# Keeping the last sums of four head pairs in SBUF until they are rotated, in place of their PSUM banks

## The chip, the cores and the metric

The kernel runs on one core of a Trainium2 chip. The metric is the time of one execution on the device, in microseconds (us). Engines are named as the profile names them: PE (TensorE matmul), DVE (VectorE), ACT (ScalarE), POOL (GpSimd) and SP (SyncE, which here only issues DMAs). SBUF is the on-chip memory that all of them read; PSUM has eight banks of 128 x 512 fp32, which PE writes and from which DVE and ACT read.

## What is computed

The reference is two gated blocks, each a cross attention and a feed-forward, on x of 8 x 256 tokens by 1024. The change touches one stage of the second attention, the queries:

```python
q = (query @ wq).reshape(bs, s, N_Q_HEADS, D_K).transpose(0, 2, 1, 3)   # 32 heads of 128
q = _rope(q)                                                           # x*cos + rot(x)*sin
```

`query` is the layer-normalised x (2048 x 1024), `wq` is 1024 x 4096. Everything is fp32 in and out; each fp32 product is made of three matmuls on split high and low parts.

## The kernel before, in words

Each engine has its own program, and the programs meet only in semaphores. `weave` interleaves the stages; the query stage, written once as `qp_schedule` and played by one class per engine, runs from 1021 to 1657 us of the profile. Before it comes the first feed-forward (names f0), after it the attention proper (names at).

The 32 heads are taken two at a time (a pair, 16 of them), once for each half of the tokens: pairs 0 to 15 for the first half, 16 to 31 for the second. A pair's query projection is one step of a Strassen-Winograd scheme, so seven products i = 0 to 6, of 12 matmuls each (`product`, the matmuls are lines 150 to 152 in the helper `three`), each into one PSUM bank. The banks are used in a ring of eight (`qp_bank`), so a product waits until the bank of the product eight places before it is read for the last time (`qp_emptied`).

`sum` adds the products up. ACT copies product 0 into c11 (line 2140). DVE adds product 1 into c12 (2163), 2 into c21 (2166), 3 into c12 (2169), and at line 2174 products 3, 4, 5, 6 give the four result quarters. c11, c12, c21 and c22 are SBUF tiles, two of each, pair modulo 2. Where line 2174 writes is told by `qp_sum`: for the last two pairs an SBUF tile of the pair, for product 3 of a coupled pair c22, otherwise back into the product's own bank.

`turn(pair, tn, part)` is the rotary embedding of one token half-block (tn 0: the quarters 4 and 5; tn 1: 6 and 3). It is six DVE instructions of 128 x 512: two products of the upper quarter with cosine and sine (2188, 2189), two of the lower one (2192, 2194, which write back over the quarters), a difference (2196) and a sum (2198) into qp_r. SP then stores qp_r. The tables qp_rope and the result qp_r lie in SBUF. So a turn reads, beside SBUF, whatever place `qp_sum` gave.

Most pairs are worked through one by one. Pairs (0, 1), (14, 15), (16, 17) and (30, 31) are coupled: their products alternate, pair by pair, because the x operands arrive then (at the begin) or are exchanged for the other token half (14 to 17). In the same stretches DVE splits the x operands (`expand`, line 2150, 128 x 1024, both inputs in SBUF). A block's turns with tn 0 are queued on DVE behind product 5's sums, those with tn 1 behind product 6's; DVE takes them in this order:

```python
if i > 4 and block[-1] < LASTP:
    for pair in block:
        for part in range(3):
            do.turn(pair, i - 5, part)
```

POOL prepares the weights of the products to come, six ahead (`prepare`): it forms the sums and differences of the weight blocks (2214, 2216, 2224, 2228) and the low parts (2220), all from SBUF to SBUF.

Of the kernel before, what the change touches and what calls it, by code (L numbers as in the profile page):

```python
# [92 lines left out]
class Signals:  # L93
# [14 lines left out]
    def inc(self, name, key, step=1):  # L108
        if self.counting:
            assert (name, key) not in self.value, (name, key)  # L110
            self.total[name] = self.total.get(name, 0) + step
            self.value[name, key] = self.total[name]
        return self.sem(name), step
# [4 lines left out]
    def at(self, name, key):  # L118
        if self.counting:
            return self.sem(name), 1  # L120
        return self.sem(name), self.value[name, key]
# [41 lines left out]
def flamingo(nc, x, ctx, ctxT, mask, gates, w0T, b0, agT, bT, gb, wq, wk, wv, wo,  # L163
             w1T, b1, enc, coef, cmask, tab, four, rope, ident, out):
    es = ExitStack()
    with es:
        sig = Signals(nc, es)
        at, inc, landed = sig.at, sig.inc, sig.landed
# [16 lines left out]
        def place(name, kb, shape, dt=F):  # L185
            return nc.alloc_sbuf_tensor_at(name, shape, dt, offset=BASE + int(1024 * kb))
# [1757 lines left out]
        NP = H // 2  # L1944
        LASTP = 2 * NP - 1
# [4 lines left out]
        Q_ORDER = [(pair, i) for block in Q_BLOCKS for i in range(7) for pair in block]  # L1950
        Q_TURNS = [(pair, tn) for block in Q_BLOCKS for tn in range(2) for pair in block]
        Q_COUPLED = [pair for block in Q_BLOCKS for pair in block if len(block) > 1]
        qp_ring = [place(f"qp_a{i}", kb, [P, 2, 4, P], R) for i, kb in enumerate((48, 52, 60, 64, 68, 72, 201.25))]
        qp_x = [[place(f"qp_b{i}_{k}", kb, [P, 2, 2, 512], R) for k, kb in enumerate(kbs)] for i, kbs in enumerate((
            (187, 0), (155, 171), (163, 179), (8, 84), (112, 120), (128, 136), (144, 104)))]
# [11 lines left out]
        def qp_bank(pair, i):  # L1967
            j = qp_at(pair, i)
            return 5 + j % 3 if pair >= LASTP - 1 else (0, 1, 4, 5, 6, 7, 2, 3)[j % 8]

        def qp_sum(pair, i):

            if pair >= LASTP - 1 or (i == 3 and pair in Q_COUPLED):
                return {3: qp_c22, 4: qp_c11, 5: qp_c21, 6: qp_c12}[i][pair % 2][:, :]
            return BK[qp_bank(pair, i)]

        def qp_emptied(pair, i):
            if i == 0:
                return ("qp_act", ("sum", pair, 0))
            if i < 3 or pair >= LASTP - 1 or (i == 3 and pair in Q_COUPLED):  # L1980
                return ("qp_dve", ("sum", pair, i))
            return ("qp_dve", {3: ("q1", pair, 1), 4: ("q0", pair, 0), 5: ("q1", pair, 0), 6: ("q0", pair, 1)}[i])

# [89 lines left out]
        class QpTensor(Queries):  # L2073
# [3 lines left out]
            def product(self, pair, i):  # L2077
                on, b, sb = self.on, qp_bank(pair, i), pair // NP
                for e in self.spare[b]:
                    on.wait_ge(*at(*e))  # L2080
                self.spare[b] = [qp_emptied(pair, i)]
                on.wait_ge(*at("qp_act", ("w", pair, i)))
                on.wait_ge(*at("qp_pool", ("w", pair, i)))
                w = qp_ring[qp_at(pair, i) % NR]
                for k in range(2):
                    x = qp_x[i][k]
                    on.wait_ge(*at("qp_act", ("x", sb, i, k)))
                    on.wait_ge(*at("qp_dve", ("x", sb, i, k)))
                    for c in range(2):
                        m = three(self.pe, BK[b], (w[:, 0, 2 * k + c, :], w[:, 1, 2 * k + c, :]), (x[:, 0, c, :], x[:, 1, c, :]),  # L2090
                                  k + c == 0, k + c == 2)
                m.then_inc(*inc("qp_pe", ("M", pair, i)))

        class QpScalar(Queries):
# [40 lines left out]
            def sum(self, pair, i):  # L2135
                if i == 0:
                    self.on.wait_ge(*at("qp_pe", ("M", pair, 0)))
                    if pair > 1:
                        self.on.wait_ge(*at("qp_dve", ("sum", pair - 2, 6)))
                    self.act.activation(qp_c11[pair % 2][:, :], BK[qp_bank(pair, 0)], ACT.Copy).then_inc(*inc("qp_act", ("sum", pair, 0)))  # L2140

        class QpVector(Queries):
# [10 lines left out]
            def sum(self, pair, i):  # L2153

                dve, on = self.dve, self.on
                c11, c12, c21 = (a[pair % 2][:, :] for a in (qp_c11, qp_c12, qp_c21))
                if i == 0:
                    return
                m = BK[qp_bank(pair, i)]
                on.wait_ge(*at("qp_pe", ("M", pair, i)))  # L2160
                if i == 1:
                    on.wait_ge(*at("qp_act", ("sum", pair, 0)))
                    dve.tensor_tensor(c12, c11, m, ALU.add).then_inc(*inc("qp_dve", ("sum", pair, 1)))
                if i == 2:
                    on.wait_ge(*at("qp_dve", ("sum", pair, 1)))
                    dve.tensor_tensor(c21, c12, m, ALU.add).then_inc(*inc("qp_dve", ("sum", pair, 2)))
                if i == 3:
                    on.wait_ge(*at("qp_dve", ("sum", pair, 2)))
                    dve.tensor_tensor(c12, c12, m, ALU.add).then_inc(*inc("qp_dve", ("fourth", pair)))
                    on.wait_ge(*at("qp_dve", ("fourth", pair)))  # L2170
                if i == 6:
                    on.wait_ge(*at("qp_dve", ("fourth", pair)))
                if i > 2:
                    dve.tensor_tensor(qp_sum(pair, i), {3: c21, 4: c11, 5: c21, 6: c12}[i], m, ALU.add).then_inc(*inc("qp_dve", ("sum", pair, i)))  # L2174

            def turn(self, pair, tn, part):

                dve, on, n = self.dve, self.on, Q_TURNS.index((pair, tn))
                top, low, q0, q1 = (a.rearrange("p (s n) -> p s n", s=4) for a in (
                    qp_sum(pair, (4, 6)[tn]), qp_sum(pair, (5, 3)[tn]), qp_r[n % 2][0][:, :], qp_r[n % 2][1][:, :]))  # L2180
                if part == 0:
                    on.wait_ge(*at("qp_rope", 1))
                    on.wait_ge(*at("qp_dve", ("sum", pair, (5, 6)[tn])))
                    if n > 1:
                        on.wait_ge(*at(f"qp_s{n % 2}", Q_TURNS[n - 2] + (1, 1)))
                    else:
                        on.wait_ge(*at("f0_xos", (NT // 2 - 1, 5)))
                    dve.tensor_tensor(q0, top, qp_angle(0, tn), ALU.mult)  # L2188
                    dve.tensor_tensor(q1, top, qp_angle(1, tn), ALU.mult).then_inc(*inc("qp_dve", ("top", pair, tn)))  # L2189
                if part == 1:  # L2190
                    on.wait_ge(*at("qp_dve", ("top", pair, tn)))
                    dve.tensor_tensor(top, low, qp_angle(1, tn), ALU.mult).then_inc(*inc("qp_dve", ("sine", pair, tn)))  # L2192
                    on.wait_ge(*at("qp_dve", ("sine", pair, tn)))
                    dve.tensor_tensor(low, low, qp_angle(0, tn), ALU.mult).then_inc(*inc("qp_dve", ("low", pair, tn)))  # L2194
                if part == 2:
                    dve.tensor_tensor(q0, q0, top, ALU.subtract).then_inc(*inc("qp_dve", ("q0", pair, tn)))  # L2196
                    on.wait_ge(*at("qp_dve", ("low", pair, tn)))
                    dve.tensor_tensor(q1, q1, low, ALU.add).then_inc(*inc("qp_dve", ("q1", pair, tn)))  # L2198
# [1042 lines left out]
```

## Time and profile before

| | |
|---|---|
| three timed runs | 3001.97 us median (2999.51 to 3003.76) |
| the profiled execution | 3001.45 us |
| its span on the core | 2999.7 us |
| PE busy | 2963.3 us, 99% |
| DVE busy | 2013.1 us, 67% |
| ACT busy | 1282.9 us, 43% |
| POOL busy | 1368.7 us, 46% |
| granted PE clock | 1.00 in the query stage (2.4 GHz) |

Busy is the time in which an engine ran an instruction; PE with 99% has about 36 us without one, in the whole kernel. A row of a timeline has start, duration, engine, line and tiles, and in brackets how long the engine stood idle before it and for whom. Durations of neighbouring DVE rows overlap by about 0.08 us, so the step from start to start is what an instruction costs in a queue.

### The profile page before, as it was taken

Reading aid. Unit: us, or ns where it says so; the run is one execution under the profiler, and the core shown is the slowest. Engines: PE = TensorE matmul, PEld = TensorE weight load, DVE = VectorE, ACT = ScalarE, POOL = GpSimd, SP = SyncE. Lnnn points to the kernel's source line nnn. Section 1 sums busy time; section 2 is a strip of 40 time slices with the busy share of each in tenths; the row PEclk is TensorE's granted clock in tenths of the full one; section 3 lists DMA queues with packets and bytes.
Section 4 is the critical chain, followed back from the end, with each engine's and each line's share of the span. In section 5 each row is a group of like instructions: output and inputs, shape, how many; then the busy total and the mean of one; then the engine's idle time right before and its main releaser. Section 6 shows DMA issues by size and latency. Waiting matters only on the chain.

```text
span 2999.7 us, 41114 instructions
## 1 busy us (share of the span) xinstructions
PE 2963.3 (99%) x14701; PEld 2484.3 (83%) x14701; DVE 2013.1 (67%) x4714; ACT 1282.9 (43%) x2686; POOL 1368.7 (46%) x1105
## 2 busy tenths in 40 slices
PE   9999999999999999999999999999999999999999
PEld 7888878887788878887888888888888888888887
DVE  4432478888655686679666777666766676666566
ACT  4111366665322422232224565555555545544332
POOL 2422388896422577778776433322222211111254
PEclk9999999999999999999999999999999999999999
DMA  7332421212655654455444776766677666665531
GB/s 253 127 120 98 172 64 50 78 64 74 201 172 176 194 164 113 113 155 158 110 110 136 243 256 227 243 218 211 190 224 241 191 193 202 209 191 165 225 112 71
DMA packets 320661, 488.29 MB, mean 163 GB/s; under 512 B 26236, under 2 KB 155644, under 8 KB 317644
## 3 DMA queue, kind: packets, MB, share of 16 engines
q1 hardware_dynamic: 319740, 484.23, 50.8%
q8 instruction: 118, 1.93, 0.3%
q10 hardware_dynamic: 720, 1.44, 0.1%
q14 instruction: 83, 0.68, 0.1%
HBM read 324.12 MB, written 161.48 MB: 162 GB/s over the span
## 4 chain that ended last, share of the span: by engine, by line
PE 59%; DVE 4%; DMA 0%; POOL 0%; ACT 0%; issue 0%; SPq 0%; DVEq 0%; ACTq 0%
PE PB L150 18%; PE PB L151 18%; PE PB L152 18%; PE PB L2400 4%; DVE qp_b L2150 1%; PE PB L2825 0%; DVE PB L2192 0%; DMA qp_raw<-in_wq 0%; DVE qp_r L2198 0%; DVE PB L2174 0%; DVE qp_c L2194 0%; DVE at_bi L2506 0%; DVE qp_r L2188 0%; DVE qp_r L2189 0%; DVE at_ptl L2539 0%
## 5 line engine op out<-in xcount | busy, mean ns | idle before, releaser
L2562 POOL TENSOR_TENSOR at_ql<-at_qf,at_qh 128x512 fp32r<-128x512 f32 x128 | 166.2, 1299 | 843.9 <-ACT at_qh L2440 843.9
L2447 ACT ACTIVATE at_ss<-at_ss,at_sm,at_bs 128x256 f32<-128x256 f32 x512 | 301.9, 591 | 318.1 <-DVE at_sm L2523 318.1
L150 PE MATMUL PB<-at_woh,at_ah 128*128 128x512 f32 x1024 | 400.8, 391 | 0.6 <-DVE at_al L2545 0.6
L151 PE MATMUL PB<-at_wol,at_ah 128*128 128x512 f32 x1024 | 400.2, 391 | 0.0
L152 PE MATMUL PB<-at_woh,at_al 128*128 128x512 f32 x1024 | 399.4, 390 | 0.0
L2553 DVE SCALAR_TENSOR_TENSOR at_xt<-PB,gt,at_xt 128x512 f32<-128x512 f32 x256 | 192.1, 751 | 255.7 <-PE PB L152 255.7
L150 PE MATMUL PB<-qp_b,qp_a 128*128 128x512 f32 x896 | 349.4, 390 | 7.2 <-DVE qp_r L2196 2.7
L152 PE MATMUL PB<-qp_b,qp_a 128*128 128x512 f32 x896 | 348.7, 389 | 0.0
L151 PE MATMUL PB<-qp_b,qp_a 128*128 128x512 f32 x896 | 348.7, 389 | 0.0
L2220 POOL TENSOR_TENSOR qp_a<-qp_raw,qp_a 128x512 fp32r<-128x512 f32 x192 | 259.2, 1361 | 100.6 <-ACT qp_a L2112 97.9
L2112 ACT ACTIVATE qp_a<-qp_raw 128x512 fp32r<-128x512 f32 x192 | 113.4, 626 | 295.3 <-POOL qp_raw L2224 162.6
L2459 ACT ACTIVATE at_pth<-PB 128x512 fp32r<-128x512 f32 x256 | 139.3, 596 | 231.8 <-PE PB L2400 231.8
L152 PEld LDWEIGHTS PB<-at_woh,at_al 128*128 128x128 f32 x1024 | 192.5, 188 | 41.1
L150 PEld LDWEIGHTS PB<-at_woh,at_ah 128*128 128x128 f32 x1024 | 193.1, 189 | 37.6 <-ACT at_ah L2470 0.8
L151 PEld LDWEIGHTS PB<-at_wol,at_ah 128*128 128x128 f32 x1024 | 193.0, 188 | 35.2
L150 PEld LDWEIGHTS PB<-qp_b,qp_a 128*128 128x128 f32 x896 | 168.2, 188 | 44.7 <-DVE qp_r L2196 3.5
L152 PEld LDWEIGHTS PB<-qp_b,qp_a 128*128 128x128 f32 x896 | 168.2, 188 | 35.1
L151 PEld LDWEIGHTS PB<-qp_b,qp_a 128*128 128x128 f32 x896 | 168.2, 188 | 34.7
L2539 DVE TENSOR_TENSOR at_ptl<-PB,at_pth 128x512 fp32r<-128x512 f32 x256 | 164.8, 685 | 39.5 <-ACT at_pth L2459 39.5
L2519 DVE CUSTOM_DVE_ANT_0 at_ss<-PB,at_bi 128x256 f32<-128x256 f32 x512 | 185.6, 419 | 0.8 <-PE PB L152 0.6
L150 PE MATMUL PB<-at_kh,at_qh 128*128 128x256 f32 x512 | 155.9, 305 | 0.0
L2533 DVE TENSOR_SCALAR at_ss<-at_ss,at_sm 128x256 f32<-128x256 f32 x512 | 150.7, 358 | 4.5
(314 smaller groups left out, 7579.3 us busy)
## 6 DMA issues: line engine op xcount, KB each, us to landing
at_woh<-wod SPq DMA_DIRECT2D x48, 1024.0 KB, 6.9
at_wol<-wod SPq DMA_DIRECT2D x48, 1024.0 KB, 9.5
qp_raw<-in_wq SPq DMA_DIRECT2D x32, 1024.0 KB, 5.4
qd<-qp_r SPq DMA_DIRECT2D x256, 128.0 KB, 2.5
at_qf<-qd SPq DMA_DIRECT2D x128, 256.0 KB, 3.4
at_rawo<-in_wo SPq DMA_DIRECT2D x32, 512.0 KB, 5.0
wod<-at_woh SPq DMA_DIRECT2D x16, 1024.0 KB, 5.5
wod<-at_wol SPq DMA_DIRECT2D x16, 1024.0 KB, 6.3
```

The lines of the kernel that those rows point to most:

```text
L150: pe.matmul(o, ah, bh, start=start, stop=False)
L151: pe.matmul(o, ah, bl, start=False, stop=False)
L152: return pe.matmul(o, al, bh, start=False, stop=stop)
L2220: pool.tensor_tensor(qp_part(pair, i, 1), qp_weight(pair, i), asf(qp_part(pair, i, 0)), ALU.subtract).then_inc(*inc("qp_pool", ("w", pair, ...
L2400: m = pe.transpose(PB[1][:, 512 * k + P * c:512 * k + P * c + P], at_ss[s][:, c, P * k:P * k + P], idt[:, :])
L2447: m = act.activation(at_ss[s][:, c, :], at_ss[s][:, c, :], ACT.Exp, bias=z[:, 4 + c:5 + c], scale=at_bs[:, qn % 2, 8 + 2 * b + c % 2:9 + 2 ...
L2459: self.act.activation(at_pth[:, k, :], BK[2 + k], ACT.Copy).then_inc(*inc("at_act", ("pt", u, k)))
L2519: dve.tensor_tensor_reduce(out=at_ss[s][:, c, :], in0=PB[0][:, L * c:L * c + L], in1=at_bi[qn % 2][:, 2 * b + c % 2, :], scale=1.0, scalar ...
L2533: dve.tensor_scalar(at_ss[s][:, c, :], at_ss[s][:, c, :], z[:, 12 + c:13 + c], None, ALU.mult).then_inc(*inc("at_dve", ("weight", u, c)))
L2539: self.dve.tensor_tensor(at_ptl[:, k, :], BK[2 + k], asf(at_pth[:, k, :]), ALU.subtract).then_inc(*inc("at_dve", ("pt", u, k)))
L2553: self.dve.scalar_tensor_tensor(out=xt, in0=BK[6 + p % 2], scalar=gt[:, 2:3], in1=xt, op0=ALU.mult, op1=ALU.add).then_inc(*inc("at_dve", ( ...
L2562: self.pool.tensor_tensor(at_ql[n % 3][:, :], at_qf[n % 2][:, :], asf(at_qh[n % 3][:, :]), ALU.subtract).then_inc(*inc("at_pool", ("q", n)))
```

## The change

A tuple `Q_KEPT` names the pairs 0, 1, 14, 15 and the last two, 30 and 31. For those, `qp_sum` now gives the SBUF tiles c22, c11, c21 and c12, where it did so before for 30 and 31 (and, of the coupled pairs, for product 3). A bank of such a pair is then free with the sum that reads it, and not with the turn's last reading. Since c11, c12 and c21 hold results until the turn is over, the pair two further on (which has the same tiles) waits for it: ACT's copy for q0 of tn 0, DVE's sums 1 and 3 for q0 and q1 of tn 1. No instruction is added, removed or moved.

```diff
+        Q_KEPT = (0, 1, NP - 2, NP - 1, LASTP - 1, LASTP)
...
         def qp_sum(pair, i):
 
-            if pair >= LASTP - 1 or (i == 3 and pair in Q_COUPLED):
+            if pair in Q_KEPT or (i == 3 and pair in Q_COUPLED):
                 return {3: qp_c22, 4: qp_c11, 5: qp_c21, 6: qp_c12}[i][pair % 2][:, :]
             return BK[qp_bank(pair, i)]
 
         def qp_emptied(pair, i):
             if i == 0:
                 return ("qp_act", ("sum", pair, 0))
-            if i < 3 or pair >= LASTP - 1 or (i == 3 and pair in Q_COUPLED):
+            if i < 3 or pair in Q_KEPT or (i == 3 and pair in Q_COUPLED):
                 return ("qp_dve", ("sum", pair, i))
...
                     if pair > 1:
-                        self.on.wait_ge(*at("qp_dve", ("sum", pair - 2, 6)))
+                        self.on.wait_ge(*at("qp_dve", ("q0", pair - 2, 0) if pair - 2 in Q_KEPT else ("sum", pair - 2, 6)))
...
                 on.wait_ge(*at("qp_pe", ("M", pair, i)))
+                if i in (1, 3) and pair - 2 in Q_KEPT:
+                    on.wait_ge(*at("qp_dve", (("q0", "q1")[i // 2], pair - 2, 1)))
```

On DVE, the last sums of the couple (0, 1) and the first turn of pair 0. Before (c110 and c210 are c11 and c21 of the even pair, c111 and c211 of the odd one, PB0 and PB2 hold banks):

```order
950 L2174 TENSOR_TENSOR PB0<-qp_c110_187,PB0 128x512 [waits qp_pe]
951 L2174 TENSOR_TENSOR PB0<-qp_c111_188,PB0 128x512 [waits qp_pe]
952 L2174 TENSOR_TENSOR PB2<-qp_c210_191,PB2 128x512 [waits qp_pe]
953 L2174 TENSOR_TENSOR PB2<-qp_c211_192,PB2 128x512 [waits qp_pe]
954 L2188 TENSOR_TENSOR qp_r00_195<-PB0,qp_rope_186 128x512 [waits f0_xos,qp_dve,qp_rope]
955 L2189 TENSOR_TENSOR qp_r01_196<-PB0,qp_rope_186 128x512
956 L2192 TENSOR_TENSOR PB0<-PB2,qp_rope_186 128x512 [waits qp_dve]
957 L2194 TENSOR_TENSOR PB2<-PB2,qp_rope_186 128x512 [waits qp_dve]
958 L2196 TENSOR_TENSOR qp_r00_195<-qp_r00_195,PB0 128x512
```

The same place of DVE in the changed kernel (its line numbers are 4 higher here):

```order
950 L2178 TENSOR_TENSOR qp_c110_187<-qp_c110_187,PB0 128x512 [waits qp_pe]
951 L2178 TENSOR_TENSOR qp_c111_188<-qp_c111_188,PB0 128x512 [waits qp_pe]
952 L2178 TENSOR_TENSOR qp_c210_191<-qp_c210_191,PB2 128x512 [waits qp_pe]
953 L2178 TENSOR_TENSOR qp_c211_192<-qp_c211_192,PB2 128x512 [waits qp_pe]
954 L2192 TENSOR_TENSOR qp_r00_195<-qp_c110_187,qp_rope_186 128x512 [waits f0_xos,qp_dve,qp_rope]
955 L2193 TENSOR_TENSOR qp_r01_196<-qp_c110_187,qp_rope_186 128x512
956 L2196 TENSOR_TENSOR qp_c110_187<-qp_c210_191,qp_rope_186 128x512 [waits qp_dve]
957 L2198 TENSOR_TENSOR qp_c210_191<-qp_c210_191,qp_rope_186 128x512 [waits qp_dve]
958 L2200 TENSOR_TENSOR qp_r00_195<-qp_r00_195,qp_c110_187 128x512
```

The order and the count are the same; the places have changed. A sum reads one SBUF tile and one bank as before and writes SBUF; the turn's instructions had a bank among their inputs and now have two inputs in SBUF.

## Rows read from the trace of the kernel before

**Rows 1.** The page: the span, and PE's busy time, share and instructions.

```profile
span 2999.7 us, 41114 instructions
...
PE 2963.3 (99%) x14701; PEld 2484.3 (83%) x14701; DVE 2013.1 (67%) x4714; ACT 1282.9 (43%) x2686; POOL 1368.7 (46%) x1105
```

**Rows 2.** Timeline of PE, the query stage's waits: start, us, instruction, idle before.

```profile
1094.73 0.50 PE L150 MATMUL PB<-qp_b,qp_a 128*128 128x512 f32 x1 [2.30 <-DVE qp_r L2198]
...
1348.81 0.50 PE L150 MATMUL PB<-qp_b,qp_a 128*128 128x512 f32 x1 [0.82 <-DVE qp_r L2196]
1353.68 0.50 PE L150 MATMUL PB<-qp_b,qp_a 128*128 128x512 f32 x1 [1.85 <-DVE qp_r L2196]
...
1364.28 0.50 PE L150 MATMUL PB<-qp_b,qp_a 128*128 128x512 f32 x1 [2.14 <-DVE qp_c L2163]
```

**Rows 3.** Timeline of DVE, from the first turn of pair 0 on.

```profile
1059.87 0.68 DVE L2188 TENSOR_TENSOR qp_r<-PB,qp_rope 128x512 f32<-128x512 f32 x1
...
1063.71 0.68 DVE L2188 TENSOR_TENSOR qp_r<-PB,qp_rope 128x512 f32<-128x512 f32 x1
...
1068.76 0.68 DVE L2188 TENSOR_TENSOR qp_r<-PB,qp_rope 128x512 f32<-128x512 f32 x1
...
1070.08 1.79 DVE L2192 TENSOR_TENSOR PB<-qp_c,qp_rope 128x512 f32<-128x512 f32 x1
1071.90 1.66 DVE L2194 TENSOR_TENSOR qp_c<-qp_c,qp_rope 128x512 f32<-128x512 f32 x1
1073.48 0.68 DVE L2196 TENSOR_TENSOR qp_r<-qp_r,PB 128x512 f32<-128x512 f32 x1
...
1075.18 0.68 DVE L2188 TENSOR_TENSOR qp_r<-PB,qp_rope 128x512 f32<-128x512 f32 x1
...
1081.94 0.68 DVE L2163 TENSOR_TENSOR qp_c<-qp_c,PB 128x512 f32<-128x512 f32 x1
...
1094.00 0.68 DVE L2198 TENSOR_TENSOR qp_r<-qp_r,PB 128x512 f32<-128x512 f32 x1
```

**Rows 4.** Timeline of POOL beside the turns with tn 1 of pair 0.

```profile
1070.01 3.00 POOL L2220 TENSOR_TENSOR qp_a<-qp_raw,qp_a 128x512 fp32r<-128x512 f32 x2
1072.97 1.74 POOL L2214 TENSOR_TENSOR qp_s<-qp_raw 128x512 f32<-128x512 f32 x1
```

**Rows 5.** All instructions on qp_c, by form: ns min/median/max, first and last start.

```profile
L2194 DVE TENSOR_TENSOR qp_c<-qp_c,qp_rope x10: 691/1654/1702, 1071.9 to 1752.7; 128x512 f32<-128x512 f32 x10
...
L2192 DVE TENSOR_TENSOR PB<-qp_c,qp_rope x6: 699/1522/1787, 1070.1 to 1386.5; 128x512 f32<-128x512 f32 x6
L2188 DVE TENSOR_TENSOR qp_r<-qp_c,qp_rope x4: 684/684/693, 1660.6 to 1742.9; 128x512 f32<-128x512 f32 x4
```

**Rows 6.** Timeline of DVE, from the first turn of pair 14 on.

```profile
1332.12 0.68 DVE L2188 TENSOR_TENSOR qp_r<-PB,qp_rope 128x512 f32<-128x512 f32 x1
...
1339.81 2.91 DVE L2150 TENSOR_TENSOR qp_b<-qp_in,qp_b 128x1024 fp32r<-128x1024 f32 x2
...
1343.84 0.68 DVE L2188 TENSOR_TENSOR qp_r<-PB,qp_rope 128x512 f32<-128x512 f32 x1
...
1350.59 0.70 DVE L2192 TENSOR_TENSOR PB<-qp_c,qp_rope 128x512 f32<-128x512 f32 x1
...
1354.63 9.00 DVE L2150 TENSOR_TENSOR qp_b<-qp_in,qp_b 128x1024 fp32r<-128x1024 f32 x4
1363.55 1.27 DVE L2163 TENSOR_TENSOR qp_c<-qp_c,PB 128x512 f32<-128x512 f32 x2
```

**Rows 7.** Timeline of POOL beside it.

```profile
1351.20 1.27 POOL L2220 TENSOR_TENSOR qp_a<-qp_raw,qp_a 128x512 fp32r<-128x512 f32 x1 [3.59 <-ACT qp_a L2112]
...
1358.17 7.84 POOL L2220 TENSOR_TENSOR qp_a<-qp_raw,qp_a 128x512 fp32r<-128x512 f32 x4
```

**Rows 8.** Busy us (x instructions) of PE, PEld, DVE, ACT, POOL in the turns' two stretches.

```profile
1059.80:1081.95 22.15, 22.15 (x98) 18.04 (x98) 21.87 (x28) 7.02 (x13) 20.14 (x16) 1.00 0.36 73
1332.10:1354.70 22.60, 19.93 (x87) 15.86 (x86) 22.32 (x30) 12.20 (x18) 14.06 (x12) 1.00 0.62 162
```

## The prediction, made before the changed kernel ran

> **What bounds the kernel now.** I read the page first: PE is busy 99% of the span [rows 1]. A change off PE can give back only PE's idle time, but whatever makes PE wait longer is paid in full. So the second view was PE's timeline in the query stage, looking for brackets with idle time. There are four of weight [rows 2]: 2.30 us at 1094.73, then 0.82, 1.85 and 2.14 us between 1348 and 1365, together 7.1 us. All four wait for DVE. This is the most that the change can gain.
>
> Third, DVE's timeline before each wait, to see what it was late with. At the first place DVE runs without a pause from the first turn of pair 0 at 1059.87 to 1094.00 [rows 3], where L2198 is q1 of pair 2's turn tn 1, and PE starts 0.05 us after that instruction's end. This product, (3, 4), wants the bank of (2, 3). Pair 2 is not kept, so this wait is not removed; everything that DVE does between 1059.87 and 1094.68 stands in front of it. At the second place the waits at 1348.81 and 1353.68 are for q0 of the turns of pairs 14 and 15, whose banks the change frees. The last, at 1364.28, is for the sum 1 of pair 16 (L2163, first of two from 1363.55 [rows 6]), which is queued behind all turns of 14 and 15 and four L2150. It stays too.
>
> Fourth, how long one DVE instruction takes by where its inputs lie. A turn with bank inputs steps evenly: six instructions from 1059.87 to 1063.71, 3.84 us or 0.64 each [rows 3]. With two inputs in SBUF there are two prices. The four L2188 at the kernel's tail take 0.684 us, so two SBUF inputs are not dear in themselves. L2194 on c22 has a median of 1.654 and a maximum of 1.702, L2192 from c22 goes from 0.699 to 1.787 [rows 5]. The cheap case of L2192 is that at 1350.59 [rows 6], in a gap in which POOL had been idle for 3.59 us until 1351.20 [rows 7]. The dear ones, 1.79 and 1.66 us at 1070.08 and 1071.90 [rows 3], lie beside a POOL that works without a gap; POOL's two instructions take 3.00 us there and the next 1.74 [rows 4]. In between, at 1073.48, an instruction with a bank input takes 0.68 again, with POOL still running. So an instruction of DVE with both inputs in SBUF and one of POOL take turns, and an instruction with one input in a bank goes past.
>
> **The change part by part.** No instruction is added. The sums (L2174) read one bank as before; only their target moves, and L2163, which reads a bank and writes an SBUF tile, takes 0.68 us [rows 3], as the turns on banks do. I put them at 0, with a bound of some hundredths of a us each way.
>
> The turns of pairs 0, 1, 14 and 15 are eight, 48 instructions. Now 12 of them read two SBUF inputs (L2192, L2194 and L2198 of tn 1, four turns); after the change all 48 do. Beside a working POOL I price one at 1.66 us, the row at 1071.90, so a turn at 6 x 1.66 = 9.96 us.
>
> First place. The turns with tn 0 take 3.84 us each now, so 2 x (9.96 - 3.84) = 12.2 more. Those with tn 1 take 6.42 (1068.76 to 1075.18) and 6.76 (1075.18 to 1081.94) [rows 3], so 19.92 - 13.18 = 6.7 more. Sum 18.9 if each one meets POOL. POOL is busy 20.14 of 22.15 us there [rows 8], 91%; its gaps and the moment when its ring of seven weight buffers is full, while PE stands, lower this. I take 85%: 16 us. Bounds: 0 (no meeting) and 18.9. PE now has no slack at 1094.73, it waits already, so the 16 us pass to it whole. PE will stand earlier as well: product (3, 2) wants the bank of (2, 1), freed by the sum that now starts at 1081.94 and would start at 1098.
>
> Second place. Turns with tn 0 now take 1332.12 to 1339.81, 7.69 us for two, so 19.92 - 7.69 = 12.2 more; those with tn 1 take 10.79 us for two (1343.84 to 1354.63 [rows 6]), so 9.1 more, 21.4 in all if each meets POOL. But POOL is busy only 14.06 of 22.60 us, 62%, with 12 instructions [rows 8]. By the share it would be 13.3 us. By the count: each POOL instruction can be met once, some 5 of the 12 are met now (the slow ones of tn 1 and one L2150), 7 are left, 7 x 1.06 = 7.4 (1.06 is from 1.70, the row's upper value, less 0.64). I take 9 us, nearer to the count, because a DVE that takes longer finds no more POOL work than there is until PE goes on. Bounds: 0 and 21.4. The wait at 1364.28 is for DVE, so this too passes whole. The two bank waits that go, 0.82 and 1.85 us, give nothing, since PE then stands at the later one, for a DVE that is later still.
>
> The new waits: ACT's copy of (2, 0) into c11 waits for q0 of pair 0's turn tn 0. Queued behind it on ACT are the weight copies of products to come; DVE reaches q0, its fifth instruction, about 5 x 1.02 = 5 us later than now, which costs at most a us or two of the lead of six products. The waits before DVE's sums 1 and 3 are for DVE's own earlier instructions, in queue order already: 0. SP's stores of qp_r come later with the turns, and the weight load behind them with them; a load is asked for seven products before its use, so I put this at 0, with up to some us if that cover is gone.
>
> Sum: 16 + 9 = 25 us on the profiled execution's 3001.45 us (span 2999.7), so 3026.5. The median of the runs, 3001.97, lies 0.5 above the profiled one. I predict 3026 us. Bounds of all: 7.1 us faster if nothing is dearer and every wait goes, 40 us slower if every instruction meets POOL.
>
> The row at 1071.90 shows DVE and POOL alternating with 1.66 us for a pair. The Trainium skill, "SBUF — State Buffer", section "Who interferes with whom", says that a DVE instruction with two SBUF inputs contends with a GpSimd instruction that reads SBUF, for the whole of the instruction, and that one with a single SBUF input does not contend. It speaks against this change, and the trace agrees on both kinds. By its "whole instruction" a meeting would cost the full length of a POOL instruction, 1.27 us [rows 7] beside 0.64, so 1.91 for a DVE instruction, and the sum would be about 30 us; the rows say 1.66, and I go by them.
>
> **The rivals.**
> A, the forecast: 18 to 34 us slower, 3019 to 3035.
> B, the meetings starve themselves. PE stands, so POOL's ring stays full and POOL is idle for half of the turns. Half of the first place (9) and a third of the second (3) give 12 us, 3013; it covers 3008 to 3019. For it: at 1351.20 POOL was idle 3.59 us in just this way. Against it: in the first place POOL is the busier side.
> C, POOL falls behind as well. Each meeting lengthens its instruction, by 1.74 - 1.27 = 0.47 or less [rows 4, 7]; 40 of them cost it up to 19 us, and PE waits for weights on top of DVE. 25 + 15 gives 3042, from 3035 on. Against it: PE waits for no weights now.
> D, the change does what it says and DVE is not slowed: the banks are free with the sums, 0.82 + 1.85 go and with luck all 7.1 us; 2994 to 2999. It would need SBUF inputs at 0.68 us beside a busy POOL. The tail's rows speak for it, those at 1070 against it.
> E, DVE is slowed but the wait at 1094.73 is not behind it, and time stays within 6 us. Against it is the unbroken row of DVE work up to 1094.
>
> **How the numbers follow.** A 0.65, B 0.16, C 0.08, D 0.06, E 0.05. A measurement of this kernel can tell about 0.2%, 6 us, from no change. Faster by more than that needs D at its best, 0.03; within it are the rest of D and E, 0.08; slower 0.89. The range 3009 to 3037 takes in A, most of B and the near end of C, and leaves out D, E and the far end of C, under 0.2.
>
> **What would show it.** In the profile after: the turns of pairs 0, 1, 14, 15 (L2192 to L2202 there) with inputs from qp_c at a median near 1.65 us between 1060 and 1100 and mixed between 1335 and 1380; the sum 1 of pair 2 (L2167) starting near 1098 in place of 1081.94; PE idle of about 18 us before (3, 4), in two or three waits for qp_c and qp_r, and about 14 us at the second place; POOL's instructions beside the turns at 1.6 to 1.75 us. Nothing after 1400 us should be changed but shifted. I am wrong if the turns stay near 0.68 us beside a working POOL (then D), if PE waits for POOL or ACT at these places (C), or if the turns are dear but PE's total wait in the stage stays under some 15 us (B).

## The result, and the profile after

| | before | after |
|---|---|---|
| timed runs, median | 3001.40 us (2999.51 to 3003.76, 5 runs) | 3027.42 us (3027.07 to 3029.36, 5 runs) |
| profiled execution, its span | 3001.45, 2999.7 us | 3027.07, 3025.3 us |

The ratio after to before is 1.0088, with a 95% interval of 1.0077 to 1.0099: the change makes the kernel 26 us slower. Predicted were 3026 us and a range of 3009 to 3037. Line numbers of the changed kernel are as before up to 1952; ACT's lines and `expand` (2152) are 2 higher; DVE's sum (2167 to 2178 in place of 2163 to 2174), its turn (2192 to 2202 in place of 2188 to 2198) and POOL's lines are 4 higher.

The page of the changed kernel: same counts, 24 us more of DVE, 7 of POOL, 8 of PE.

```profile
span 3025.3 us, 41115 instructions
...
PE 2971.2 (98%) x14701; PEld 2489.1 (82%) x14701; DVE 2036.8 (67%) x4714; ACT 1282.9 (42%) x2686; POOL 1375.5 (45%) x1105
```

PE's timeline in the query stage, all stops of weight, beside those of [rows 2]:

```profile
1066.38 0.47 PE L150 MATMUL PB<-qp_b,qp_a 128*128 128x512 f32 x1 [1.03 <-POOL qp_a L2224]
...
1097.68 0.79 PE L150 MATMUL PB<-qp_b,qp_a 128*128 128x512 f32 x1 [9.23 <-DVE qp_c L2167]
1109.75 0.79 PE L150 MATMUL PB<-qp_b,qp_a 128*128 128x512 f32 x1 [4.68 <-DVE qp_r L2202]
1110.34 0.63 PE L151 MATMUL PB<-qp_b,qp_a 128*128 128x512 f32 x1
1110.77 0.63 PE L152 MATMUL PB<-qp_b,qp_a 128*128 128x512 f32 x1
...
1368.69 0.50 PE L150 MATMUL PB<-qp_b,qp_a 128*128 128x512 f32 x1 [2.71 <-DVE qp_c L2178]
...
1377.02 0.47 PE L150 MATMUL PB<-qp_b,qp_a 128*128 128x512 f32 x1 [2.59 <-ACT qp_a L2114]
1388.64 0.80 PE L150 MATMUL PB<-qp_b,qp_a 128*128 128x512 f32 x1 [4.29 <-DVE qp_c L2167]
```

7.1 us of waits have become some 25 (the first row's 1.03 us for POOL included). The stop at 1094.73 now ends at 1109.75, 15.0 us later, with one more before it; that at 1364.28 ends at 1388.64, 24.4 later. And a matmul takes 0.63 us behind the long stops, with 0.43 from start to start.

DVE's timeline at the first place, against [rows 3], the first turn of pair 0 and the start of pair 1's, the start of the turns with tn 1, and the end of the stretch:

```profile
1060.20 0.77 DVE L2192 TENSOR_TENSOR qp_r<-qp_c,qp_rope 128x512 f32<-128x512 f32 x1
1060.89 1.77 DVE L2193 TENSOR_TENSOR qp_r<-qp_c,qp_rope 128x512 f32<-128x512 f32 x1
1062.70 1.67 DVE L2196 TENSOR_TENSOR qp_c<-qp_c,qp_rope 128x512 f32<-128x512 f32 x1
1064.40 0.69 DVE L2198 TENSOR_TENSOR qp_c<-qp_c,qp_rope 128x512 f32<-128x512 f32 x1
1065.01 1.77 DVE L2200 TENSOR_TENSOR qp_r<-qp_r,qp_c 128x512 f32<-128x512 f32 x1
1066.70 1.78 DVE L2202 TENSOR_TENSOR qp_r<-qp_r,qp_c 128x512 f32<-128x512 f32 x1
1068.41 1.78 DVE L2192 TENSOR_TENSOR qp_r<-qp_c,qp_rope 128x512 f32<-128x512 f32 x1
...
1079.80 1.83 DVE L2192 TENSOR_TENSOR qp_r<-qp_c,qp_rope 128x512 f32<-128x512 f32 x1
...
1095.75 0.68 DVE L2200 TENSOR_TENSOR qp_r<-qp_r,qp_c 128x512 f32<-128x512 f32 x1
1096.35 0.68 DVE L2202 TENSOR_TENSOR qp_r<-qp_r,qp_c 128x512 f32<-128x512 f32 x1
1096.96 0.67 DVE L2167 TENSOR_TENSOR qp_c<-qp_c,PB 128x512 f32<-128x512 f32 x1
```

POOL beside it:

```profile
1060.39 1.74 POOL L2224 TENSOR_TENSOR qp_a<-qp_raw,qp_a 128x512 fp32r<-128x512 f32 x1
1062.20 1.62 POOL L2228 TENSOR_TENSOR qp_raw<-qp_s,qp_raw 128x512 f32<-128x512 f32 x1
1064.63 3.31 POOL L2224 TENSOR_TENSOR qp_a<-qp_raw,qp_a 128x512 fp32r<-128x512 f32 x2 [0.81 <-ACT qp_a L2114]
...
1092.02 3.26 POOL L2224 TENSOR_TENSOR qp_a<-qp_raw,qp_a 128x512 fp32r<-128x512 f32 x2
1104.45 1.28 POOL L2218 TENSOR_TENSOR qp_s<-qp_raw 128x512 f32<-128x512 f32 x1 [9.16 <-DMA qp_raw<-in_wq]
```

The pattern is the one of [rows 3] and [rows 4], now on 19 of the 24 instructions of the four turns: about 1.7 us from start to start beside a working POOL, both engines lengthened. The row at 1064.40 is one of the exceptions and fits the pattern: POOL's instruction of 1062.20 has ended at 1063.82 and its next starts at 1064.63, and DVE takes 0.69. The same at 1095.75, after POOL's last instruction at 1095.28. The sum 1 of pair 2 starts at 1096.96 in place of 1081.94.

### The profile page after: what moved, and what is told of

Read it like the earlier page. It is cut to its first block, busy times and chain, and to the rows that moved or that the text cites. A ratio compares the mean times of both kernels' runs of the same rounds, so it can differ in the third digit from the quotient of the medians.

```text
span 3025.3 us, 41115 instructions
## 1 busy us (share of the span) xinstructions
PE 2971.2 (98%) x14701; PEld 2489.1 (82%) x14701; DVE 2036.8 (67%) x4714; ACT 1282.9 (42%) x2686; POOL 1375.5 (45%) x1105
## 4 chain that ended last, share of the span: by engine, by line
PE 59%; DVE 5%; DMA 1%; issue 0%; ACT 0%; POOL 0%; SPq 0%; DVEq 0%; ACTq 0%
PE PB L150 18%; PE PB L151 18%; PE PB L152 18%; PE PB L2404 4%; DVE qp_b L2152 1%; DVE qp_r L2193 0%; PE PB L2829 0%; DVE qp_r L2192 0%; DVE qp_r L2202 0%; DVE qp_c L2196 0%; DVE qp_c L2198 0%; DMA qp_raw<-in_wq 0%; DVE qp_r L2200 0%; DVE at_bi L2510 0%; DVE f1st L2942 0%
## 5 line engine op out<-in xcount | busy, mean ns | idle before, releaser
L150 PEld LDWEIGHTS PB<-qp_b,qp_a 128*128 128x128 f32 x896 | 170.2, 190 | 64.3 <-DVE qp_c L2167 14.4
L152 PEld LDWEIGHTS PB<-qp_b,qp_a 128*128 128x128 f32 x896 | 170.3, 190 | 35.9
L151 PEld LDWEIGHTS PB<-qp_b,qp_a 128*128 128x128 f32 x896 | 170.4, 190 | 35.3
```

The lines of the kernel that those rows point to most:

```text
L150: pe.matmul(o, ah, bh, start=start, stop=False)
L151: pe.matmul(o, ah, bl, start=False, stop=False)
L152: return pe.matmul(o, al, bh, start=False, stop=stop)
```

## The experiments

The theory: a DVE instruction with two SBUF inputs waits for a POOL instruction that reads SBUF, and the reverse; the change turns 36 more instructions into that kind at two places where DVE is what PE waits for. Rivals: two SBUF inputs are dear in themselves; the new waits hold an engine up; the early free banks change PE's order of work for the worse. A second theory came from the profile after: PE's clock is lower for some us behind the long stops, and that is a cost of its own. The kernel before was timed anew beside each group of experiments, so its median is 3001.98, 3001.16 or 3002.91 us below.

**Each place alone.**

```diff
-        Q_KEPT = (0, 1, NP - 2, NP - 1, LASTP - 1, LASTP)
+        Q_KEPT = (0, 1, LASTP - 1, LASTP)                    # e1_first
+        Q_KEPT = (NP - 2, NP - 1, LASTP - 1, LASTP)          # e2_second
```

> Only pairs 0 and 1 (beside 30 and 31) are kept in SBUF; pairs 14 and 15 as before. Theory (dearer turns, then a slow PE clock behind the stall): 15.0 us of later DVE plus 2.3 us of slow matmuls, so 17 us slower than before, near 3018.5, and nothing at 1330 to 1400 us. Rival (the first place is off the bound): under 6 us. Rival (one common cause such as the longer program or the memory layout): all 26 us here too.

Measured: 3018.13 us against 3001.98, ratio 1.0053 (1.0041 to 1.0066), 16.2 us slower, as the theory said.

> Only pairs 14 and 15 (beside 30 and 31) are kept. Theory: the rest of the change's cost, 7.0 us of later DVE plus 2.8 us of slow matmuls behind the stall, so 8 to 10 us slower than before, near 3011; the two together give the whole change. If the places interact (the first shifting what meets what at the second), the two differences do not add up to 26.

Measured: 3009.91 against 3001.98, ratio 1.0028 (1.0018 to 1.0038), 7.9 us slower. 16.2 + 7.9 = 24.1, within the intervals the 26.0 of both. The two places stand for the whole, the first with two thirds.

**The free bank taken back.** The sums stay in SBUF, but PE waits for the banks until the turns are over.

```diff
-            if i < 3 or pair in Q_KEPT or (i == 3 and pair in Q_COUPLED):
+            if i < 3 or pair >= LASTP - 1 or (i == 3 and pair in Q_COUPLED):      # in qp_emptied
```

> The changed kernel, but PE waits for a kept pair's banks until its turns are over, as before the change. The SBUF inputs of the turns stay. Theory (the inputs are the cost, the early free bank gives nothing because PE stands for DVE in any case): within 3 us of the changed kernel, 3025 to 3030. Rival (the early bank gives back a part, the inputs cost more than was seen): 3033 or more. Rival (the early start of PE is what collides): near 3001.

Measured: 3021.52 against 3001.98, ratio 1.0067 (1.0052 to 1.0082). None of the three: it is 19.5 us slower than before, where the changed kernel is 26.0 slower. So three quarters of the loss come with the inputs alone, and the early bank makes it worse by some 6 us, not better. The size is rough: the two kernels were not timed side by side, and the intervals of their ratios overlap. PE's timeline of this kernel, its two long stops at the first place and its last one at the second:

```profile
1076.21 0.52 PE L150 MATMUL PB<-qp_b,qp_a 128*128 128x512 f32 x1 [4.86 <-DVE qp_r L2200]
...
1094.72 0.79 PE L150 MATMUL PB<-qp_b,qp_a 128*128 128x512 f32 x1 [5.05 <-DVE qp_r L2200]
...
1384.96 0.50 PE L150 MATMUL PB<-qp_b,qp_a 128*128 128x512 f32 x1 [2.73 <-DVE qp_c L2167]
```

PE stands earlier (at the bank of pair 0's quarter) and its last stop at the first place ends at 1094.72, not at 1109.75. The slow matmuls behind that stop run while DVE is still catching up, and PE reaches the critical product (3, 4) when its bank is just free. In the changed kernel PE runs ahead through the freed banks, then stands for DVE twice, the second time at (3, 4) itself, and the slow matmuls behind that stop are on the path. DVE's stretch is also 1 us shorter here (1059.46 to 1107.94 against 1060.20 to 1109.70) and begins 0.7 us earlier. At the second place DVE's part is the same in both (7.1 and 7.0 us), but here the last stop is 2.73 us long and the clock stays at 1.00 behind it, where the changed kernel has a stop of 4.29 us and a fall of the clock. Behind the second place this kernel is 20.7 us later than the one before and the changed one 27.2, so 6.5 us apart. Of its 27.2 us the changed kernel lost 5.2 behind its two last stops, at the lower clock (2.4 and 2.8, worked out below); this one lost 0.3 there. That the early bank costs mainly by way of the clock is read from one execution of each and was not tried by itself.

**The changed waits alone**, on the kernel before:

```diff
-                        self.on.wait_ge(*at("qp_dve", ("sum", pair - 2, 6)))
+                        self.on.wait_ge(*at("qp_dve", ("q0", pair - 2, 0) if pair - 2 in (0, 1, NP - 2, NP - 1) else ("sum", pair - 2, 6)))
...
+                if i in (1, 3) and pair - 2 in (0, 1, NP - 2, NP - 1):
+                    on.wait_ge(*at("qp_dve", (("q0", "q1")[i // 2], pair - 2, 1)))
```

> The kernel before with the change's two new waits alone (ACT's copy for q0 of tn 0, DVE's sums 1 and 3 for q0 and q1 of tn 1, of the pair two before, for pairs 0, 1, 14, 15). Sums stay in their banks. Theory: the waits cost nothing, within 2 us of before. Rival (ACT held by the wait delays the weight copies queued behind it, and PE waits for weights): 3 to 10 us slower.

Measured: 3002.71 against 3001.98, ratio 1.000 (0.9991 to 1.0009). The waits cost nothing that shows: by the interval, under 3 us. ACT's is not even a further wait. The kernel before waits at the same place for sum 6 of the pair two before, and DVE takes that sum behind q0 of tn 0, so the edit lets ACT's copy go earlier. For pair 16, first before, then with the edit:

```profile
1343.42 0.60 ACT L2140 ACTIVATE qp_c<-PB 128x512 f32<-128x512 f32 x1 [3.13 <-DVE PB L2174]
...
1341.99 0.58 ACT L2140 ACTIVATE qp_c<-PB 128x512 f32<-128x512 f32 x1
```

The profiled execution with the edit has two short waits of PE that the one of before lacks, 0.98 us for POOL at 1376.76 and 0.50 us for ACT at 1380.23. No run shows where they come from.

**POOL without its reads.** For the weights of pairs 0 to 5 and 13 to 19 POOL writes zeros in place of the low parts, sums and differences, in the kernel before (e5) and in the changed one (e6).

```diff
+                op = (lambda o, a, b, f: pool.memset(asf(o), 0.0)) if pair <= 5 or NP - 3 <= pair <= NP + 3 else pool.tensor_tensor
...
-                pool.tensor_tensor(qp_part(pair, i, 1), qp_weight(pair, i), asf(qp_part(pair, i, 0)), ALU.subtract).then_inc(
+                op(qp_part(pair, i, 1), qp_weight(pair, i), asf(qp_part(pair, i, 0)), ALU.subtract).then_inc(
```

> The kernel before, with POOL's work on the weights of pairs 0 to 5 and 13 to 19 (low parts, sums and differences) left out: POOL writes zeros to the same tiles and reads nothing from SBUF. Theory (a DVE instruction with two SBUF inputs waits for a POOL instruction that reads SBUF): the slow L2192, L2194, L2198 and L2150 become fast, 0.69 and 1.2 us, DVE's backlog shrinks and PE's 7 us of waits in the stage go, so 5 to 8 us faster than before, 2994 to 2997. Rival (POOL's writes collide too): as before, 3001.

Measured: 2991.28 against 3001.16, ratio 0.9966 (0.9952 to 0.9979).

> The changed kernel with the same work of POOL left out (zeros written, nothing read, for the weights of pairs 0 to 5 and 13 to 19). Theory: the change's whole cost is the meeting with POOL's reads, so this is within 2 us of the same edit on the kernel before, 2994 to 2998, and all turns take 0.69 us an instruction. Rival (two SBUF inputs are dear in themselves, or the later write to c11, c12 and c21 holds someone): 20 to 26 us slower than the same edit on the kernel before.

Measured: 2991.40 against 3001.16, ratio 0.9965 (0.9951 to 0.9979). This is the deciding pair. With POOL's reads the change costs 26 us, without them 0.1. Both are faster than the kernel before by 10 us, and PE has no stop for DVE over 0.2 us left in the stage: the kernel before had been paying for such meetings too. The forms of the turns in the changed kernel with the zeros (min, median and max ns), against [rows 5]:

```profile
L2198 DVE TENSOR_TENSOR qp_c<-qp_c,qp_rope x14: 691/691/694, 1058.7 to 1743.3; 128x512 f32<-128x512 f32 x14
L2202 DVE TENSOR_TENSOR qp_r<-qp_r,qp_c x14: 681/684/687, 1059.9 to 1752.3; 128x512 f32<-128x512 f32 x14
L2192 DVE TENSOR_TENSOR qp_r<-qp_c,qp_rope x12: 680/684/692, 1056.7 to 1733.4; 128x512 f32<-128x512 f32 x12
```

and two neighbours in its timelines of DVE and of POOL, where POOL writes zeros while DVE reads two SBUF tiles:

```profile
1065.59 0.68 DVE L2192 TENSOR_TENSOR qp_r<-qp_c,qp_rope 128x512 f32<-128x512 f32 x1
...
1065.87 0.53 POOL L2212 MEMSET qp_s<- 128x512 f32 x1
```

The largest of these DVE durations is 0.694 us, and some of the instructions lie beside a memset, so a POOL instruction that only writes does not hold them. A limit of this test: a memset takes 0.53 us and not 1.29, so POOL is also idle for most of the time, and the times alone can't tell reads from mere work of POOL; the rows beside a memset can. The same rows show that two inputs in SBUF and a result in c11, c12 or c21 are not dear in themselves.

**DVE late without any meeting.** The kernel before, with the first instruction of pair 0's turn, on a bank, done 20 times more (e7) or 5 times more (e9).

```diff
+                    for k in range(20 if (pair, tn) == (0, 0) else 0):     # 5 in e9_delay_small
+                        dve.tensor_tensor(q0, top, qp_angle(0, tn), ALU.mult).then_inc(*inc("qp_more", k))
+                        on.wait_ge(*at("qp_more", k))
```

> The kernel before with DVE delayed at the first place and nothing else: the first instruction of pair 0's turn (one bank and one SBUF input, 0.6 to 0.75 us a step) is done 20 times more. Theory (DVE's backlog passes one to one to PE, and the stop adds some 2 us of slow PE clock): the added 12 to 15 us and 2 us, 14 to 17 us slower than before, with POOL's instructions near 1.29 us. Rival (DVE has slack and the change cost by POOL's lengthening): under 6 us slower.

Measured: 3016.94 against 3001.16, ratio 1.0051 (1.0036 to 1.0067), 15.8 us slower (by the interval, 11 to 20). In its trace:

```profile
1061.12 14.46 DVE L2189 TENSOR_TENSOR qp_r<-PB,qp_rope 128x512 f32<-128x512 f32 x20
...
1078.27 0.68 DVE L2199 TENSOR_TENSOR qp_r<-qp_r,PB 128x512 f32<-128x512 f32 x1
...
1096.19 0.68 DVE L2163 TENSOR_TENSOR qp_c<-qp_c,PB 128x512 f32<-128x512 f32 x1
```

```profile
1062.74 1.29 POOL L2227 TENSOR_TENSOR qp_raw<-qp_s,qp_raw 128x512 f32<-128x512 f32 x1
1064.84 2.55 POOL L2223 TENSOR_TENSOR qp_a<-qp_raw,qp_a 128x512 fp32r<-128x512 f32 x2 [0.81 <-ACT qp_a L2112]
```

POOL runs at 1.29 us beside DVE's bank instructions, and 14.5 us of DVE make the sum 1 of pair 2 14.25 us late and the span 13.4 us longer (3013.1 against 2999.7); this execution was the fastest of the four. So DVE's lateness at this place does pass to the end nearly in full, by itself, whatever made it. The 2 us for the clock are not in this trace: the clock fell behind a stop of 9.72 us at 1079.00, but PE stands for DVE once more behind it, 3.00 us until 1108.99, and after that stop the clock stayed up.

> The kernel before, with DVE delayed by 5 steps of 0.72 us (3.6 us) at the first turn of pair 0, on a bank and an SBUF input. Theory: PE waits 3.6 us more, in one stop of near 6 us, behind which its clock falls for some 2 us: 4 to 6 us slower than before, 3005 to 3007. Rival (PE had slack for small delays): no change.

Measured: 3004.70 against 3002.91, ratio 1.0009 (1.0000 to 1.0019), 1.8 us slower: less than expected. In the profiled execution the wait before 1095.55 grew by only 0.7 us, from 2.30 to 2.98. DVE's stretch began 1.3 us earlier there (an operand had come sooner), and the turns with tn 1, shifted against POOL, took 11.7 us in place of 13.2. In this execution a part of the delay was swallowed by meeting less, and the clock did not fall behind these stops.

**Looking for something better than before.** e8 keeps one more sum, product 3 of pair 2, in c22, so that the product which stood at 1094.73 has its bank.

```diff
-            if pair >= LASTP - 1 or (i == 3 and pair in Q_COUPLED):
+            if pair >= LASTP - 1 or (i == 3 and pair in Q_COUPLED + [2]):          # in qp_sum, and alike in qp_emptied
```

> The kernel before, with product 3 of pair 2 alone put into c22 as well (so that the bank of (2, 3) is free with its sum and not with q1 of the turn tn 1). Theory: the wait of 2.30 us at 1094.73 goes, for 1 to 3 us more of DVE time in the turn (three instructions with two SBUF inputs) which nobody waits for; 1 to 2.5 us faster than before, 2999 to 3001. Rival (the added meetings bring back a wait of the same length): no change, or 1 us slower.

Measured: 2998.76 against 3001.16, ratio 0.9990 (0.9982 to 0.9999): 2.4 us faster, just clear of 1, and as the theory said. In its trace the wait at 1094.73 is gone. The later ones are 0.92, 2.63 and 2.14 us, 0.9 us more than before. The profiled execution, 3002.65 us, is the slowest of its eleven, so it can't show where the 2.4 us were gained.

e10 goes the other way about and lets the turn read a bank where it had read c22: ACT copies it there.

```diff
+            def turn(self, pair, tn, part):                                        # QpScalar
+                if part == 0 and qp_swap(pair, tn):                                # tn 1 of 0, 1, 14 to 17
+                    self.on.wait_ge(*at("qp_dve", ("top", pair, tn)))
+                    self.act.activation(qp_sum(pair, 6), qp_sum(pair, 3), ACT.Copy).then_inc(*inc("qp_act", ("moved", pair)))
...
+                if part and qp_swap(pair, tn):                                     # QpVector.turn
+                    top, low = low, top
```

> The kernel before, with the meetings it had already made fewer: in the coupled blocks (0, 1), (14, 15) and (16, 17), ACT copies quarter 3 from c22 into the bank of quarter 6 once the turn has read that bank, DVE reads the copy, and the two pairs' turns with tn 1 take their parts alternately so that the copy is hidden. Of the three instructions of such a turn with two SBUF inputs one is left. Theory: about 3.5 us less of DVE time at the first place and 1 to 2 at the second, the wait of 2.30 us at 1094.73 goes and the later ones shrink: 2 to 5 us faster than before, 2996 to 2999. Rival (DVE waits for the copy as long as it saves): no change.

Measured: 3000.22 against 3002.91, ratio 0.9993 (0.9984 to 1.0002): 2.7 us faster, but unclear. The step worked where it was aimed: PE's waits for DVE are gone at both places, and the sum 1 of pair 2 starts at 1078.29. In their place stands one for POOL:

```profile
1348.67 0.76 PE L150 MATMUL PB<-qp_b,qp_a 128*128 128x512 f32 x1 [3.47 <-POOL qp_a L2236]
```

## Why the prediction was right

The time, the places and the mechanism came as written; the parts of the sum did not all have their size, and one was missing.

**First place, 16 us predicted.** DVE was 15.0 late at (3, 4), 109.70 - 94.68 in the trace's last digits. The turns with tn 0 took 18.4 us (1060.20 to 1078.60) in place of 7.7, so 10.7 more, of the 12.2 possible; those with tn 1 17.2 (1079.80 to 1096.96) in place of 13.2, so 4.0 of 6.7. The stretch also began 0.3 later. POOL's gaps were where I put them; a step was 1.70 us, a little over my 1.66. The share of 85% was 78%. PE stood 14.9 us there (1.03, 9.23 and 4.68), where I had named about 18.

**Second place, 9 us predicted.** Measured 7.0: the shift of PE grows from 17.4 (L2167 at 1321.88 against L2163 at 1304.51) to 24.4 at the stop of 1388.64. The turns with tn 0 took 7.5 us more. Those with tn 1 took 0.9 us less than before, not more, since POOL stood idle for 8.44 us until 1375.40. It waited for ACT's copies of weights, and these were queued behind ACT's copy of an x operand, for which ACT stood 7.49 us until its DMA had landed at 1372.80. By the program that DMA waits for a split of DVE's, which here ended at 1368.04. DVE itself, being late, had kept POOL idle:

```profile
1369.16 0.68 DVE L2192 TENSOR_TENSOR qp_r<-qp_c,qp_rope 128x512 f32<-128x512 f32 x1
...
1374.33 0.69 DVE L2196 TENSOR_TENSOR qp_c<-qp_c,qp_rope 128x512 f32<-128x512 f32 x1
...
1375.67 1.76 DVE L2200 TENSOR_TENSOR qp_r<-qp_r,qp_c 128x512 f32<-128x512 f32 x1
```

This is what the rival B forecast, POOL idle during the turns, at half of one place, though it came by a DMA and not by a full ring of weight buffers. The count of POOL's instructions (7.4) came nearer than its busy share (13.3), at this one place. PE stood 9.6 us here (2.71, 2.59 and 4.29), where I had named about 14.

**The term that was missing: PE's clock.** Behind a long stop the matmuls start 0.43 us apart in place of 0.23, for about a dozen of them. Busy times and, third from the end, the granted clock, of the changed kernel:

```profile
1110.00:1115.00 5.00, 5.00 (x13) 3.90 (x14) 2.37 (x4) 1.35 (x3) 3.76 (x3) 0.52 0.91 204
1115.00:1120.00 5.00, 5.00 (x24) 4.12 (x23) 2.75 (x5) 1.27 (x2) 3.87 (x3) 1.00 1.03 432
...
1389.00:1394.00 5.00, 5.00 (x13) 3.84 (x13) 4.93 (x9) 0.00 (x0) 1.36 (x2) 0.50 0.76 240
```

0.50 is the lower level, 1.2 GHz. At the first place this is 17.4 - 15.0 = 2.4 us, at the second 27.2 - 24.4 = 2.8 us (27.2 is the shift of the same sums at 1572.36 before and 1599.55 after). The prediction has no term for the clock and says that the stops pass whole; they pass with some more. The fall behind the stop of 9.23 us cost nothing, since PE stood for DVE again behind it. So DVE gave 22.0 us, not 25, and the clock 5.2, together 27.2. Of those 1.6 are missing at the end for a reason that is none of the change's: the profiled execution of before had a clock of 0.91 in one stretch where the other had 1.00.

```profile
2140.00:2160.00 20.00, 18.12 (x88) 15.05 (x87) 16.54 (x40) 9.56 (x25) 5.30 (x4) 0.91 0.61 198
```

That 3026 was met to 1.4 us is therefore partly luck: two terms too high by 3 us, one of 5 not seen.

**The free banks, 0 predicted.** With the SBUF inputs in place they cost some 6 us (e3); with POOL out of the way the whole change makes no difference (0.1 us, e5 and e6). I had argued that PE would stand at the later wait in any case; I had not seen that where it stands decides whether the slow matmuls are on the path.

**The changed waits, 0 to 2 us predicted:** under 3 us, and not told from 0 (e4). I had read ACT's wait as a further one, with q0 later than now; it takes the place of one for a still later instruction. In the changed kernel ACT does come late in the second place, PE waits 2.59 us for it at 1377.02, and for POOL 1.03 us at 1066.38. These are what I had named as a sign of being wrong, for rival C. But both lie ahead of a later stop for DVE and cost nothing that can be told apart, and POOL's busy time grew by 6.8 us in all, not by the 19 of C.

The rule of the Trainium skill cited in the prediction ("SBUF — State Buffer", section "Who interferes with whom") holds here. That two SBUF inputs contend with a GpSimd instruction that reads SBUF, and not with one that only writes it, is what the kernel before and e6 show: 1.66 us beside a read, at most 0.694 beside a memset. That a single SBUF input does not contend is what e7 shows, with POOL at 1.29 us. By the "whole instruction" of the same page of the Trainium skill (section "SBUF: two separate sides") a meeting is priced at 1.91 us, as in the prediction, and the rows say 1.70.

## What to carry to other kernels

Before an operand is moved from PSUM to SBUF to free a bank, count which two-input DVE instructions will then have both inputs in SBUF, and look whether GpSimd is reading SBUF beside them: here each one that met such a read went from 0.60 to 1.70 us, on the very engine that PE waited for. The number of the other engine's instructions in the stretch bounds the number of meetings; here it came nearer than the busy share. An earlier free bank is worth something only if a wait for that bank ends last, and a stop of PE should be priced with the slow matmuls behind it, if no other stop follows that swallows them.

## What the runs showed of the hardware that was not expected

- PE's clock fell to its lower level behind all ten stops of 3.2 us and more that these traces have in the stage (3.20 in e2, 3.47 in e10, 4.29, 4.68 and 9.23 in the changed kernel, 4.71 and 8.75 in e1, 4.86 and 5.05 in e3, 9.72 in e7). Where no other stop followed, the fall cost 2.4 and 2.8 us in the changed kernel. Behind stops of 2.1 to 3.0 us it fell in 7 cases of 21, and the length alone did not decide: the kernel before did not fall after 2.30 us at 1094.73, and the kernel with the changed waits alone, otherwise the same there, did after 2.33 us; it fell after 2.14 us in e8, at 1363.62, and not after 3.00 us in e7. The case after 2.33 us:

```profile
1094.73 0.80 PE L150 MATMUL PB<-qp_b,qp_a 128*128 128x512 f32 x1 [2.33 <-DVE qp_r L2200]
1095.33 0.63 PE L151 MATMUL PB<-qp_b,qp_a 128*128 128x512 f32 x1
```

- Taking POOL's reads out of 13 of 32 pairs gained 10 us where the stage's waits were 7.1 us in all. In the two profiled executions the gain is 8.7 us. Put side by side, matmul for matmul, they show 8.2 of it at the four stops of [rows 2]: each is worth some 0.27 us more than the idle time in its bracket. The timed 10 us have an interval of 6 to 14, so the rest lies within it.
